# Edge scores with a row of edges per partition, and unrolled layer norms

## The reference

```
h = x @ Wn.T + bn                                 # x is the layer norm of the nodes
e = edge_attr @ We.T + be
a = leaky_relu(sum((h[src] + e) * attn), 0.01)    # one score per edge
m = segment_max(a, dst);  a = exp(a - m[dst])
out = relu(segment_sum(h[src] * a / segment_sum(a, dst)[dst], dst))
```

## Time and profile before

| | |
|---|---|
| Median of 3 runs | 4746.15 us (4743.47 to 4758.92) |
| Profiled execution | 4745.81 us, span 4744.0 us |
| PE busy | 3527.1 us, 74% |
| DVE busy | 3048.8 us, 64% |
| ACT busy | 1980.5 us, 42% |
| POOL busy | 799.1 us, 17% |
| Mean DMA rate | 89 GB/s |

### The profile page before, as it was taken

The page is one execution under the profiler, slowest core; times in us unless marked ns, Lnnn a source line. Parts: engine busy times, 40 slices in busy tenths (PEclk is TensorE's granted clock), DMA queues, the critical chain, the costliest instruction groups (busy, mean ns, idle before and its releaser), DMA issues. The chain is left out here.

```text
span 4744.0 us, 72228 instructions
## 1 busy us (share of the span) xinstructions
PE 3527.1 (74%) x21084; PEld 2873.1 (61%) x21085; DVE 3048.8 (64%) x6675; ACT 1980.5 (42%) x5195; POOL 799.1 (17%) x685
## 2 busy tenths in 40 slices
PE   2211299998994999993699999989999477896391
PEld 1211155555884899982577777777777366775161
DVE  4699788884115200013999999999999518996412
ACT  1000014686001344431566666666666266662020
POOL 1565300000003400042011111111111000002414
PEclk9655599999995999995799999999999788997596
DMA  1899402355432202123011111111110403320323
GB/s 58 158 197 196 105 28 111 166 216 242 151 125 74 83 29 75 52 69 135 33 42 41 41 41 41 41 43 51 49 41 10 158 30 130 115 101 9 93 70 111
DMA packets 202091, 422.06 MB, mean 89 GB/s; under 512 B 12560, under 2 KB 157188, under 8 KB 185236
## 3 DMA queue, kind: packets, MB, share of 16 engines
q1 hardware_dynamic: 178964, 350.71, 23.3%
q0 software_dynamic: 14976, 44.58, 3.1%
q10 hardware_dynamic: 8064, 25.69, 1.9%
HBM read 296.14 MB, written 124.79 MB: 89 GB/s over the span
## 5 line engine op out<-in xcount | busy, mean ns | idle before, releaser
L1324 PE MATMUL gat_agg<-f_XN,gat_A 128*128 128x257 f32 x5000 | 1132.5, 385 | 22.6 <-DVE gat_A L1429 22.6
L1324 PEld LDWEIGHTS gat_agg<-f_XN,gat_A 128*128 128x128 f32 x5000 | 955.7, 193 | 163.7 <-DVE gat_A L1429 23.2
L1258 ACT ACTIVATE kept_X<-kept_X,gat_s 128x128 f32<-128x128 f32 x2500 | 741.4, 387 | 481.6 <-DVE kept_X L1418 481.6
L1418 DVE SCALAR_TENSOR_TENSOR kept_X<-gat_r,gat_s 128x128 f32<-128x128 f32 x2500 | 665.1, 348 | 45.8 <-POOL gat_r L1206 45.7
L893 PE MATMUL mat_cw<-mat_join,mat_lane 128*128 128x400 f16 x2976 | 509.1, 333 | 35.3 <-issue 19.4
L2339 ACT ACTIVATE moe_exp_h<-moe_exp_hbank,moe_b1c 128x128 f32<-128x128 f32 x742 | 271.4, 368 | 547.4 <-PE moe_exp_hbank L2290 375.3
L893 PEld LDWEIGHTS mat_cw<-mat_join,mat_lane 128*128 128x128 f16 x2976 | 290.6, 98 | 254.4 <-issue 47.3
L1391 DVE CUSTOM_DVE_ANT_0 gat_junk<-gat_als,gat_absT 128x3200 bf16<-128x3200 f32 x100 | 348.4, 3484 | 24.0 <-DMA gat_als<-score_rows 15.1
L2297 PE MATMUL moe_exp_ybank<-moe_exp_w2b,moe_exp_h 128*128 128x256 f32 x1484 | 351.7, 386 | 6.3 <-issue 3.1
L1429 DVE SCALAR_TENSOR_TENSOR gat_A<-kept_X,gat_C 128x1664 f32<-128x1664 f32 x200 | 354.5, 1816 | 0.0
L2373 DVE TENSOR_TENSOR moe_exp_xgT<-moe_exp_ybank,moe_b 128x256 f32 x109 | 46.3, 425 | 460.3 <-PE moe_exp_ybank L2297 460.3
(11 more groups left out here) (367 smaller groups left out, 4642.6 us busy)
## 6 DMA issues: line engine op xcount, KB each, us to landing
gat_C<-count_matrix SPq DMA_DIRECT2D x50, 1600.0 KB, 6.2
soft_raw<-in_edge_attr_dram SPq DMA_DIRECT2D x96, 512.0 KB, 7.8
count_matrix<-mat_both SPq DMA_DIRECT2D x25, 1600.0 KB, 5.3
weight_matrix<-mat_both SPq DMA_DIRECT2D x25, 1600.0 KB, 8.8
soft_lo_rows<-src_low_bits ACTq DMA_DIRECT2D x56, 448.0 KB, 6.0
e_WT<-weight_matrix SPq DMA_DIRECT2D x13, 1600.0 KB, 6.8
sum_more<-weight_matrix SPq DMA_DIRECT2D x12, 1600.0 KB, 6.7
slot_rows<-moe_exp_xgT POOLq DMA_DIRECT2D x22, 640.0 KB, 3.9
```

The lines of the kernel that those rows point to most:

```text
L1258: last = nc.scalar.activation(w, w, ACT.Exp, bias=s02[:, t, h:h + 1])
L1324: last = nc.tensor.matmul(agg[h % 2][:, 0:D + 1], A[h % 2][:, t, :], g.XN[:, t, :], start=(t == 0), stop=(t == NT - 1))
L1418: last = nc.vector.scalar_tensor_tensor(out=work[h % 2][:, t * P:(t + 1) * P], in0=r1[:, h, :], scalar=s08[:, t, h:h + 1], in1=r2[:, h, :] ...
```

## The change

`load_attr` is new. It loads 16 edges of each row at a time, 8 KB in one piece per partition, to one of six buffers (`RAW_BUFS = 6`); 56 steps cover all edges. For the first 34 steps one more transfer of one row loads the piece of the short row. The first six steps are loaded in `edge_constants`, in SP's list between the loads of `dst` and the store of its bordered copy. POOL scales them in place during the first layer norm (`scale_early`), the other 50 in `edge_softmax`. The low bits of `src` stay on the chip: PE spreads a row of them to all partitions, ACT forms |low bits - partition| and then relu(1 - that), which is the one-hot. The comparison of the high bits becomes one DVE instruction of 25 x 784 elements in bf16, in `gnn0_project`. The order in a step on DVE is multiply, sum of attributes, sum over candidates. The attribute term is then in rows already, so that only the found term is transposed.

`project_nodes` loses its loops. Statistics are taken in groups of five tiles, a group ahead; ACT applies the norm in one instruction as `x * rstd + shift`, and writes straight to where the experts and layer 1 keep the normalised nodes and their transposes.

The diff, cut:

```diff
-def project_nodes(nc, sems, tag, X, ident, weights, width, finish, xT_all=None):
+def project_nodes(nc, sems, tag, X, ident, weights, width, finish, xn_all=None, xT_all=None, pool_work=None):
...
-            pool.wait_ge(s_rstd, 1)
-            with strides(pool, NT, UNROLL) as i:
...
-                    nc.gpsimd.tensor_tensor(xn[:, u, :], X[:, at(i + u), :].rearrange("p o d -> p (o d)"),
-                                            mv[:, at(i + u), 0].to_broadcast([P, D]), ALU.subtract).then_inc(centred, 1)
...
+            gather_stats(0)
+            for n in range(N_GROUPS):
+                if n + 1 < N_GROUPS:
+                    gather_stats(n + 1)
+                norms(n)
+                if n >= 1:
+                    finish_group(n - 1)
+            finish_group(N_GROUPS - 1)
...
+                nc.scalar.activation(xn(t), X[:, t, :], ACT.Identity, bias=shift[:, t:t + 1],
+                                     scale=rstd[:, t:t + 1]).then_inc(xn_ready, 1)
...
                 sp.dma_start(to[0:ER - 1, :], of[0:whole].rearrange("(r w) -> r w", w=EW)).then_inc(loaded, 16)
                 sp.dma_start(to[ER - 1:ER, 0:E_LAST], of[whole:N_EDGES].rearrange("(r w) -> r w", r=1)).then_inc(loaded, 16)
+            for s in range(RAW_BUFS):
+                load_attr(sp, g, attr, s)
...
-            sp.wait_ge(lo_ready, 1)
-            sp.dma_start(srclo.rearrange("(r w) -> r w", w=EW), lo_h[:, :]).then_inc(stored, 16)
...
+                nc.vector.tensor_tensor(g.pick_hi[:, :, :].rearrange("p h (c t) -> p h c t", t=2),
+                                        g.hi[:, :].rearrange("p (o c t) -> p o c t", o=1, t=2)
+                                        .to_broadcast([P, NT, CH // 2, 2]),
...
+def load_attr(sp, g, attr, s):
+
+    place, arrived = g.raw[s % RAW_BUFS], g.raw_in[s % RAW_BUFS]
+    whole = attr[0:(ER - 1) * EW, :].rearrange("(r w) d -> r w d", w=EW)
+    sp.dma_start(place[0:ER - 1, :, :], whole[:, s * AT_ONCE:(s + 1) * AT_ONCE, :]).then_inc(arrived, 16)
+    if rows_of_step(s) == ER:
+        first = (ER - 1) * EW + s * AT_ONCE
+        sp.dma_start(place[ER - 1:ER, :, :],
+                     attr[first:first + AT_ONCE, :].rearrange("(r w) d -> r w d", r=1)).then_inc(arrived, 16)
...
+    pool.wait_ge(g.raw_in[s % RAW_BUFS], landed(s))
+    nc.gpsimd.tensor_tensor(mine, mine, g.v[0:rows, :].rearrange("p (o d) -> p o d", o=1)
+                            .to_broadcast([rows, AT_ONCE, P]), ALU.mult).then_inc(g.scaled_ready, 1)
...
+            for s in range(RAW_BUFS, STEPS):
+                sp.wait_ge(ea_ready, s - RAW_BUFS + 1)
+                load_attr(sp, g, attr, s)
...
+                nc.scalar.activation(away[:, r % 2, :].rearrange("p (b e) -> p b e", b=2),
+                                     spread[r % 2][:, :].rearrange("p (b e) -> p b e", b=2)[:, :, 0:HALF],
+                                     ACT.Abs, bias=g.minus_lane[:, 0:1]).then_inc(away_ready, 1)
...
+                for b in range(2):
+                    last = nc.tensor.matmul(spread[r % 2][:, b * 512:b * 512 + HALF],
+                                            g.ident16[0:ER, r:r + 1].to_broadcast([ER, P]),
+                                            g.src_lo[:, b * HALF:(b + 1) * HALF], start=True, stop=True)
...
-                nc.vector.tensor_scalar(pick_lo[:, u, :], lo_rows[:, u, :], g.iota_p[:, 0:1], None,
-                                        ALU.is_equal).then_inc(pick_ready, 1)
...
+            for s in range(STEPS):
+                multiply(s)
+                attr_score(s)
+                look_up(s)
```

More of the change, by code:

```diff
@@ L149, in project_nodes @@
         rstd = k.sb("rstd", [P, NT])
[L150 to L159, removed]
+        shift = k.sb("shift", [P, NT])
@@ new lines, in project_nodes @@
+        xn_ring = None if xn_all is not None else k.sb("xn", [P, XN_BUFS, D])
+        xT_ring = None if xT_all is not None else k.sb("xT", [P, XT_BUFS, D])
+        turned = [k.ps(f"turned{b}", [P, 512]) for b in range(TURN_BUFS)]
+        prod = [k.ps(f"prod{b}", [P, 512]) for b in range(PROD_BUFS)]
+        stats_ready, mv_ready, var_ready = k.sem("stats_ready"), k.sem("mv_ready"), k.sem("var_ready")
+        std_ready, rstd_ready, shift_ready = k.sem("std_ready"), k.sem("rstd_ready"), k.sem("shift_ready")
@@ L164, in _, with members, span @@
+        def members(n):
+            return range(n * IN_GROUP, (n + 1) * IN_GROUP)
+        def span(n):
+            return slice(n * IN_GROUP, (n + 1) * IN_GROUP)
         @block.vector
         def _(dve):
[L167 to L182, removed]
@@ new lines, in norms, with finish_group @@
+            def norms(n):
+                dve.wait_ge(std_ready, n + 1)
+                nc.vector.reciprocal(rstd[:, span(n)], std[:, span(n)]).then_inc(rstd_ready, 1)
+                dve.wait_ge(rstd_ready, n + 1)
+                nc.vector.scalar_tensor_tensor(out=shift[:, span(n)], in0=mv[:, span(n), 0], scalar=-1.0,
+                                               in1=rstd[:, span(n)], op0=ALU.mult, op1=ALU.mult).then_inc(shift_ready, 1)
+            def finish_group(n):
+                for t in members(n):
+                    dve.wait_ge(prod_ready, t + 1)
+                    finish(t, prod[t % PROD_BUFS], xn(t)).then_inc(finished, 1)
@@ L197, in _ @@
+            gather_stats(0)
[6 more added lines that the diff above has]
+            finish_group(N_GROUPS - 1)
+        if pool_work is not None:
+            @block.gpsimd
+            def _(pool):
+                pool_work(pool)
         @block.scalar
         def _(act):
-            act.wait_ge(s_var, 1)
-            nc.scalar.activation(std[:, :], var[:, :], ACT.Sqrt).then_inc(s_std, 1)
@@ L201, in _, with root @@
[L201 to L212, removed]
+            def root(n):
+                act.wait_ge(var_ready, n + 1)
+                nc.scalar.activation(std[:, span(n)], var[:, span(n)], ACT.Sqrt).then_inc(std_ready, 1)
@@ L214, in _, with turn @@
+            root(0)
+            for t in range(NT + 2):
+                if t < NT:
+                    normalise(t)
+                    if t % IN_GROUP == 1 and t // IN_GROUP + 1 < N_GROUPS:
+                        root(t // IN_GROUP + 1)
+                if t >= 2:
+                    keep_turned(t - 2)
         @block.tensor
         def _(pe):
[L216 to L222, removed]
+            def turn(t):
+                pe.wait_ge(xn_ready, t + 1)
+                if t >= TURN_BUFS:
+                    pe.wait_ge(xT_ready, t - TURN_BUFS + 1)
@@ L239, in _, with project @@
[L239 to L243, removed]
-                project(i, UNROLL - 1)
-def edge_constants(nc, sems, g, src, dst, dpad, srclo):
+            def project(t):
+                pe.wait_ge(xT_ready, t + 1)
+                if t >= PROD_BUFS:
+                    pe.wait_ge(finished, t - PROD_BUFS + 1)
+                for c in range(KD):
+                    last = nc.tensor.matmul(prod[t % PROD_BUFS][:, 0:width], xT(t)[:, c, :], weights(c),
+                                            start=(c == 0), stop=(c == KD - 1))
+                last.then_inc(prod_ready, 1)
@@ L253, in edge_constants @@
+            for t in range(NT + 1):
+                if t < NT:
+                    turn(t)
+                if t >= 1:
+                    project(t - 1)
+def edge_constants(nc, sems, g, src, dst, dpad, attr):
     with ExitStack() as ctx:
```

308 lines of the change are left out of this document (156 added, 152 removed).

## The result

Kernel before: 4746.2 us median of four runs (4743.5 to 4758.9). Changed kernel: **4957.4 us** median of four runs (4954.3 to 4964.3). The ratio is 1.0442, with a 95% interval of 1.042 to 1.0463. The forecast of 4965 us stands 8 us above the median, and its sign is right. The profiled execution of the changed kernel took 4964.3 us, span 4962.5 us, against a span of 4744.0 us before.

A forecast was written before the change was run, and what follows sets the result against it. A step was taken as bounded by transfers in small pieces and by DVE and POOL in each other's way. 194 - 1 + 64 + 4 - 36 - 6 = +219 on 4745.8 gave 4965 us, range 4893 to 5015.

The forecast's parts named there:

- Three engines for a load of 111 rows: Attribute loads: 111 rows run on 3 of 16 DMA engines at 77 GB/s, taken as 11.5 us a step.
- The loop, +194: Loop of `edge_softmax`: transfers without a gap set the pace, 601 us against 407, +194 us, bounds +170 to +209.
- The six early loads, +64: Edge constants: SP's next store waits in the queue behind six loads, block ends at 110.4 instead of 46.0 us.
- High bits, +4: `gnn0_project`: the comparison of 19,600 elements on DVE takes 11.7 us, partly beside loads; +4 us, at worst +15.
- Norms, -36: moe0, ln1 and moe1: grouped statistics and PE's pace without POOL save 12 us each; bounds -27 to -42.
- ln0, -6: First layer norm: the gain is partly lost as POOL's six multiplications hold up DVE's small steps; -13 to +5 us.
- The store did not overtake: Rival for edge constants: a later store passes the early loads, so the +64 goes: 4901 us, chance 0.08.
- starved lists: Rival: fetching unrolled instructions shares DMA engines with loads, adding 20 to 60 us to norms and loop edges: 5000 us, chance 0.06.
- All engines carrying the loads: Rival for the attribute loads: POOL's 4.6 us a step decides, loop 247 us, total 4559 us, chance 0.09.
- The turning point: Loop of `edge_softmax`: under about 7.9 us a step it is no longer slower than before.

The follow-up runs named there:

- the swap: In PE's list the spread of row r+2 goes ahead of the sums of row r: 4955.7 us on the changed kernel, 4563.5 us with loads on all engines.
- the third experiment: The changed kernel with the six early loads, still 111 rows, moved behind the packed store in SP's list: 4937.5 us.
- The fourth experiment: The kernel before with only the new layer norms, attributes scaled in the loop as before and none in ln0: 4697.1 us.
- the last: All engines, reordered PE list, early loads behind the packed store; then epsilon added in ACT's square root and shift reading the reciprocal from PSUM: 4530.3 us.

## Why the prediction was right, step by step

**Three engines for a load of 111 rows.** Shown. Rows in the large load and GB/s: 111 gives 81, 95 gives 129 (with 16 more on all engines), 110 gives 174, 96 gives 228. The last is the pace at which buffers came free, as POOL did not wait for a load there. The number of packets below 512 bytes, from 300 to 380 us, counts the engines more directly. The changed kernel, the one with five engines without the swap, and the one with all engines and the swap have:

```profile
DMA packets 815, 6.47 MB, mean 81 GB/s; under 512 B 28, under 2 KB 28, under 8 KB 28
DMA packets 1519, 10.49 MB, mean 131 GB/s; under 512 B 243, under 2 KB 243, under 8 KB 243
DMA packets 2597, 16.65 MB, mean 208 GB/s; under 512 B 572, under 2 KB 572, under 8 KB 572
```

These are 7, 11 and 18 steps, so 4, 22 and 32 small packets a step: 3 + 1, 5 + 16 + 1 and 16 + 16, one for each engine that has a part of a load. Of the page "DMA: Bandwidth & Descriptors" of the Trainium skill, section "Why a DMA increments its semaphore by 16 and not by 1", the rule (the largest number up to 16 that divides the rows) gives 3, 5, 11 and 16: the traces agree, in order and roughly in size. 11.5 us a step was measured as 11.6 and 11.3.

**The loop, +194.** +187.5. The 6.5 us are mostly the price of a piece: 11.3 us for 111 rows and not 11.5 takes off 9 us over 50 loads, and the first multiplication of the loop came 24.4 us into the block, some 3 us later than summed (the first load was issued at 10.5 us, not 8). The load of one row, 11.63 - 11.30 = 0.33 us against 0.32, was right.

**The six early loads, +64.** The size is right (+63.5), the way there only in half. I had the store issued at 30.3 us and waiting in the queue for all six loads. In fact SP was held 10.08 us by each load from the third on and issued the store at 75.81; from there its return took 25 us more, behind what was queued. Both ways end with the last load, so the sum is the same. It differs as soon as the loads move: SP's hold cost 42 us of the block in the third experiment, where the queue alone would have cost nothing. The same page of the Trainium skill, section "Queues, rings and completion order", has each engine take its descriptors in ring order, and the 25 us agree with it.

**High bits, +4.** 10.4 us for the comparison against 11.7, and +2.7 in the sum; cover and size were right.

**Norms, -36.** -43.3, 1 us past the bound. The mechanism held, PE is the bound without POOL. Its size was off: 25 tiles went 1.17 us apart, where I took 1.27 from a place at which PE was already waiting a little.

**ln0, -6.** -0.3, inside -13 to +5. The fourth experiment shows the gain was there (-12.6) and the last that the small steps beside POOL took nearly all of it (38.5 us with both the new norm and the scalings). I had halved the stretching for PE's cover; nothing covered it, as the first shift ended only at 171.9 us, 13.4 us into the stage, and PE had no tile before it.

**The rivals.** The store did not overtake. Of starved lists nothing is seen: the loop's period is that of the load, and waits put down to issue stand on PE's weight loads, while it waited for DVE; and the same unrolled lists run at 4.06 to 4.48 us a step once the loads allow it. All engines carrying the loads: it did not happen, and the price I gave it, 4559 us, was wrong for the kernel as changed. It would have been 4712. I compared the engines' busy times per step and did not ask in which order PE's list takes rows. With that order mended the 4559 is met at 4563. The turning point that I gave, 7.9 us a step, was not measured; at 7.04 us a step softmax takes 441.7 us against 453.7, which fits it.

## What to carry to other kernels

Before a layout is chosen for its long pieces, look at how many engines its row count reaches: here 111 rows cost 357 us against 110 and one, in the kernel whose PE list was in the better order. A forecast for "the bottleneck is gone" needs the chain through the next engines with the order in their lists, not their busy times; an edit that is worth nothing under one bound can be worth 149 us under the next. And when work is moved to where an engine is idle, look at what its neighbour does there: six scalings on POOL cost 12 to 15 us wherever short DVE steps ran beside them, until one of those steps was taken away and another read one operand from PSUM.

## What the runs showed of the hardware

- *An issue can hold the issuing engine.* With a load of 111 rows SP was held 10.08 to 11.3 us by the issue of the one-row load behind it, from the third load on; with 5 engines 5.8 to 6.8 us by the large load and the one of 16 rows together, with 16 engines at most 2.4 us. Everything behind it in SP's list waits, even at the end of a block. What fills up is not shown here.
- *More engines make each piece slower.* An 8 KB piece took 0.31 us on 3 engines, 0.37 with 5, 0.62 x 16 x 8192 / 174 GB/s = 0.47 with 11, and 0.98 x 16 x 8192 / 228 GB/s = 0.56 with 16 (0.50 from 300 to 380 us, at 208 GB/s and a share of 0.80). Before, 393 GB/s were reached at 0.91 with other transfers, which is 0.30 us for 8 KB, so this is not the engines' own limit. Whether the stride of 459 KB between the pieces is the cause was not tried.
- *Which small DVE steps POOL holds up.* Beside multiplications of 4.5 us, a sum with a constant took 2.3 us, a step with two SBUF tensors 4.2 to 4.4, a cast 4.4, and each ended where a multiplication did. A reciprocal took 0.15, and the step with two tensors 0.16 once one of them was in PSUM. The page "SBUF — State Buffer" of the Trainium skill, section "SBUF: two separate sides", says that the port pair DVE shares with GpSimd is taken by a whole instruction at a time, and by DVE for two SBUF inputs or in a two-port mode. The traces agree in what they show of two inputs and of whole instructions. Whether the sum and the casts, which have one input, ran in such a mode is not shown.
